# Four scatters of a batch at one place in GpSimd's order, instead of three and one

## What is computed

```python
h = layernorm(x) * (1 + ca) + sa
Q, gate, K, V = h @ Wq ..., h @ Wk, h @ Wv        # 16 heads of 8 features, Q and K RMS-normed
attn = softmax(Q K^T / sqrt(8));  o = (attn @ V) * sigmoid(gate)
x = x + ga * (o @ Wo + bo)
h = layernorm(x) * (1 + cb) + sb
rw = softmax(h @ router_w.T);  vals, idx = top_k(rw, 2)      # 2 of 32 experts for each token
x = x + gb * sum_k vals_k * (h @ expert_weights[idx_k])
```

## Time and profile before

| | |
|---|---|
| median of three runs | 1137.25 us |
| the profiled execution | 1129.86 us |
| its span, first to last instruction | 1128.2 us |
| first part of the program (attention and routing) | to about 780 us |
| busy over the span: TensorE, VectorE, ScalarE, GpSimd | 60%, 66%, 48%, 52% |
| mean granted TensorE clock | 0.845 of full speed |

### The profile page before, as it was taken

One profiled execution on the slowest core, in us unless ns is written; L12 is line 12 of the kernel. 1 busy time (PEld: TensorE's weight loads), 2 busy tenths in 40 slices (PEclk: granted clock), 3 DMA queues, 4 the chain that ended last, 5 costly groups with the idle time before them and its releaser, 6 DMA issues. The chain is left out here.

```text
span 1128.2 us, 26188 instructions
## 1 busy us (share of the span) xinstructions
PE 675.7 (60%) x5838; PEld 432.4 (38%) x5839; DVE 741.2 (66%) x2260; ACT 536.6 (48%) x1335; POOL 584.1 (52%) x940
## 2 busy tenths in 40 slices
PE   2477887878888788788888888761356660000000
PEld 0134555545545445454455555430345550000000
DVE  5486998898898898889888889634622222333333
ACT  1255876677777777677677777640022220000000
POOL 4121456555655655665565655556222226666765
PEclk9588999899999998999999999965599995555555
DMA  2245545344544544545454453310666563333333
GB/s 60 62 127 130 128 116 143 93 114 113 133 110 106 137 113 104 128 104 124 109 124 110 113 133 99 86 43 28 227 201 203 204 194 90 98 102 94 106 98 95
DMA packets 115825, 132.72 MB, mean 118 GB/s; under 512 B 16901, under 2 KB 96613, under 8 KB 115269
## 3 DMA queue, kind: packets, MB, share of 16 engines
q1 hardware_dynamic: 96036, 91.93, 32.0%
q0 software_dynamic: 12736, 33.84, 9.4%
q10 hardware_dynamic: 7008, 6.43, 2.0%
HBM read 78.62 MB, written 52.96 MB: 117 GB/s over the span
## 5 line engine op out<-in xcount | busy, mean ns | idle before, releaser
L1144 DVE TENSOR_REDUCE negmax<-mx_ps 128x2 f32<-128x512 f32 x512 | 340.2, 684 | 77.6 <-remote 41.0
L892 ACT ACTIVATE pr<-st_ps 128x512 f32<-128x512 f32 x512 | 286.7, 597 | 51.3 <-PE st_ps L1536 45.5
L1514 PE MATMUL mx_ps<-k_aug,q_aug 126*128 126x256 bf16 x1024 | 203.4, 283 | 74.4 <-DVE negmax L1144 58.2
L1536 PE MATMUL st_ps<-q_aug,k_aug 128*128 128x256 bf16 x1024 | 176.6, 281 | 0.9 <-ACT pr L892 0.3
L1550 PE MATMUL o_ps<-pr,v_aug 128*32 128x256 f32 x2048 | 141.2, 394 | 48.0 <-ACT oT L898 25.9
L781 POOL DMA_INDIRECT yg<-ys_d,gi x128 | 124.3, 971 | 63.1 <-issue 41.1
L713 POOL DMA_INDIRECT xs_d<-h,slot x128 | 127.7, 998 | 55.6 <-DVE slot L1267 32.0
L1514 PEld LDWEIGHTS mx_ps<-k_aug,q_aug 126*128 126x128 bf16 x1024 | 77.0, 99 | 176.8 <-issue 168.2
L1536 PEld LDWEIGHTS st_ps<-q_aug,k_aug 128*128 128x128 bf16 x1024 | 96.5, 103 | 35.1 <-issue 11.8
L1550 PEld LDWEIGHTS o_ps<-pr,v_aug 128*32 128x32 f32 x2048 | 56.8, 110 | 98.1 <-issue 78.1
L1416 DVE TENSOR_SCALAR yw<-yg,p_all 128x128 f32<-128x128 f32 x64 | 16.1, 310 | 113.1 <-DMA yg<-ys_d,gi 87.4
(11 more groups left out here) (188 smaller groups left out, 1317.5 us busy)
## 6 DMA issues: line engine op xcount, KB each, us to landing
q_aug<-q_d SPq DMA_DIRECT2D x64, 192.0 KB
ys_d<-ys POOLq DMA_DIRECT2D x48, 256.0 KB, 3.0
mod_o<-mod_d SPq DMA_DIRECT2D x32, 256.0 KB
bias_p<-bias_d SPq DMA_DIRECT2D x32, 200.0 KB
q_d<-parts SPq DMA_DIRECT2D x32, 192.0 KB, 2.1
k_d<-parts SPq DMA_DIRECT2D x32, 192.0 KB, 2.1
k_aug<-k_d SPq DMA_DIRECT2D x64, 96.0 KB
xs<-xs_d ACTq DMA_DIRECT2D x48, 128.0 KB, 2.2
```

Of the source, the lines that this page charges most:

```text
L892: nc.scalar.activation(pr[:, h % PR], st_ps[score_bank(b, h)][:], ACT.Exp, scale=SCALE).then_inc(exp_d, 1)
L1144: v.tensor_reduce(negmax[:, :, h], mx_ps[h % 2][:], AX.X, ALU.max, negate=True).then_inc(mx_d, 1)
L1514: last = t_.matmul(mx_ps[h % 2][:, qc], q_aug[b.par][0:MROW, h, qc * P:(qc + 1) * P], k_aug[b.par][0:MROW, h, :], start=True, stop=True)
L1536: last = t_.matmul(st_ps[score_bank(b, h)][:, kc], k_aug[b.par][:, h, kc * P:(kc + 1) * P], q_aug[b.par][:, h, :], start=True, stop=True)
```

## The change

All four scatters of a batch are issued at one place of GpSimd's step, one step after their slots are known, right behind `low_part(b1)`. Before, the first three stood behind `max_rest` of the batch's own step, and the fourth at the very start of the next. Only GpSimd's list changes; the lists of the other engines are the same.

```diff
             def step(b0, b1, b2, b3, b4, b5, b6, b7, b8):
 
-                scatter(b7, 3)
                 copy_v(b2)
                 x_plus_bias(b4)
                 scale_wo(b4)
                 low_part(b1)
+                scatter(b7, 0)
+                scatter(b7, 1)
+                scatter(b7, 2)
+                scatter(b7, 3)
                 keep_slot(b7)
                 scale_wqkv(b0)
                 chosen(b6)
...
                 max_rest(b2)
-                scatter(b6, 0)
-                scatter(b6, 1)
                 keep_weights(b8)
-                scatter(b6, 2)
                 less_largest(b6)
                 norm_qk(b0, 0)
                 norm_qk(b0, 1)
```

## The result

| | median, us | lowest to highest | runs |
|---|---|---|---|
| before | 1137.94 | 1133.21 to 1139.79 | 4 |
| after | 1206.55 | 1204.02 to 1211.17 | 4 |

The ratio is 1.0614 (95% interval 1.0568 to 1.0661): 68.6 us slower. The prediction said 1174 us, 36 us slower, with a range of 1146 to 1218. The sign and the range held; the value was only half of the loss. The experiments were timed in three groups, each beside the kernel before on a chip of its own (medians of 1053.73, 1128.15 and 1128.18 us), and each ratio is to the kernel before of the same group.

The account below looks back on a forecast made before the run. VectorE was taken as nearest to a bound, with 2.6 us idle per step. Per step +3.0 - 0.2 - 1.6 + 0.2 = +1.4 us, over 26 steps +36: 1137.25 + 36 = 1174 us, range 1146 to 1218.

Parts of the forecast that it names:

- The fourth scatter leaves the start: Step start on GpSimd, ahead of `v_aug`: moving this scatter away is worth 0, between 0 and 0.1 us a step.
- The mask is late by 3.0: Four scatters behind the low part start GpSimd's mask 3.0 us late (2.8 to 3.8); TensorE's count and later work move too.
- The 0.2 won back: Of the mask's 3.0 us delay, 0.2 a step is recovered from VectorE's 0.65 us idle elsewhere (bounds 0 and 0.65).
- The end stop's gain of 1.6: Step end: moving three scatters away removes the 1.8 to 1.95 us stop, gaining 1.6 us a step (0 to 1.95).
- a sign of being wrong: Listed sign against the forecast: "remote" waits of 1.8 us still there, at the old place or beside the train.
- The rival that saw it coming: End stop stays or moves along with the scatters: +3.0 to +3.3 us a step, 1219 us; chance 0.20.
- The clock, +0.2: TensorE's longer pause lowers its clock more often: 0.2 us a step added, between -0.3 and 1.5.
- the clock falls in nearly every step: Rival: TensorE spends 3.4 to 6.9 us per step at the lower clock, 0.5 to 1.4 more, 1200 us; chance 0.13.
- the one with 0.52: The forecast itself: +1.4 us a step over 26 steps, 1174 us, within 1160 to 1190; chance 0.52.
- a mean clock under 0.90: Sign that the clock's term was too small: TensorE's mean clock in 200 to 640 us below 0.90.
- the faster rival: Mask hardly late and end stop gone: 1095 us with no delay, about 1135 with half of it; chance 0.08.

## Why the prediction was half right

The step falls into two stretches: from the low part's end to the mask, and from the mask round to the next low part's end. The first is the median of the traces, the second what the step leaves.

| kernel | low part to mask | mask to next low part | step, us |
|---|---|---|---|
| before | 3.0 | 18.5 | 21.5 |
| before, additions for scatters | 3.0 | 17.2 | 20.2 |
| after | 5.95 | 18.55 | 24.5 |
| after, additions for scatters | 5.9 | 18.25 | 24.2 |
| after, TensorE kept busy | 5.95 | 17.0 | 23.0 |

- *The fourth scatter leaves the start: 0.* Right: moving it alone gave 0.997, a few us at most.
- *The mask is late by 3.0.* Right in place and size: 5.93 against 3.03 us, and TensorE waits 3.7 us a step for it. At full clock nearly all of it enters the step: 22.97 (TensorE kept busy) less 20.19 is 2.8, the holding included. The 0.2 won back were fair.
- *The end stop's gain of 1.6.* The size stands between the 1.3 that the additions give at the least and 2.0 at the most. The mechanism was not the forecast's: the stop left the step's end, but it was not removed, it moved. Results are now held beside the train, 2.9 us a step for `onT` (55.9 in 19 cases), where TensorE and nearly all others wait for the mask anyway. By the prediction's own list that was a sign of being wrong. The rival that saw it coming priced it at 1219 us, as if the held results would cost in full at the new place too; the traces give them 0.3, not clear of noise.
- *The clock, +0.2.* This is the term that was mis-sized, and most of the missing half. The prediction put it so: "I add 0.2 us a step, between -0.3 and 1.5". It measured 1.5 a step between two traces, 1.2 between two medians and 1.0 between two ratios, near the upper bound. The table shows how it hid the gain: without the stop, mask to low part would be 17.0 to 17.2 us; the half clock behind the pause puts it back to 18.55, as long as before with the stop.

With the terms of the traces: 2.5 for the late mask at full clock (2.8 less the 0.3), 0.3 for the holding, 1.5 for the clock, 1.3 of gain: 2.5 + 0.3 + 1.5 - 1.3 = +3.0, and 24.50 - 21.51 is 2.99. They must add up so, since each term is a difference between the same steps; the sum divides the loss and doesn't check it. With a gain of 2.0 the late mask and the holding would have 3.5 together, and the clock would keep its 1.5. The kernel before loses something to the clock too (0.96 to 0.97); that share lies within the gain. A check from outside is the forecast's sum with the clock of the medians, 1.4 - 0.2 + 1.2 = 2.4 a step: 26 times that is 62 us, and the medians stand 68.6 apart, 2.6 a step. The first two profiled executions, 1129.86 and 1207.40 us, stand 77.5 apart; their steps, (702.8 - 162.4) / 25 = 21.62 and 24.34 us, make 68 of it over the 25 steps between masks.

That the range held is in part luck: the sum gave 36 us and steps of 22.7 to 23.4 us, where the traces have 24.3 to 24.5, and its upper end came from the prices of the rivals. Of the cases laid out, the one that came true is "the clock falls in nearly every step", at 1200 us and 0.13, and not the one with 0.52. The row for it was there: in the step of the earlier trace rows with the clock at 0.85, a pause of 1.9 us was followed by the fall, and I took the price of a longer pause from the average over all steps. I should have asked what TensorE does while it waits: in the kernel before it stops at the step's end for less than 2 us with work on either side, after the change it stands for 3.7 us in each step, and then the low clock lies on the matmuls that release everyone. The sign that the prediction gave for this, a mean clock under 0.90, was set wrongly too: the mean is 0.91, since the longer step dilutes 3.3 us at 0.52.

The Trainium skill, page "TensorE: Matmul & The Clock Gate", section "Why this matters for your kernels", warns against such pauses between bursts of matmuls. The runs agree: 0.91 with the pause and 1.00 with the same wait filled, 24.50 and 22.97 us a step. The Trainium skill, page "DMA: Bandwidth & Descriptors", section "Anatomy of one DMA — SWDGE (gpsimd) path", calls the making of descriptors small; on GpSimd's row each indirect DMA is 0.95 to 1.03 us and the next one comes 1.26 to 1.34 us later, and the faster rival that leaned on it fell with that.

## What to carry to other kernels

Room on an engine is a pocket ahead of one instruction, with a size: 2.1 us took one scatter for nothing, and four overran it by 2.9, which nearly all entered the step, since TensorE's list had no slack behind the mask. When a change makes TensorE wait in each step, add to the wait itself what the low clock costs behind it (here 1.0 to 1.5 us on top of 2.8), and read it from a stretch at the low level, not from an average; a few matmuls without use in the wait gave it back here. A stand-in for an instruction has neighbours of its own: look at what the other engines' instructions beside it take before its step is used as a base. And when a stall is taken away, ask which buffers, landings or held results wait at the new place: both this change and the spread of the scatters took the stop from the step's end and met waits elsewhere.

## What was not expected of the hardware

- While a train of indirect DMAs is issued on GpSimd, results of TensorE reach ScalarE and VectorE late (transposes issued at 529.51, copied at 533.16), with waits that no instruction accounts for. GpSimd additions of 1.29 to 1.48 us at the same places show none. Three close together at the step's end did it, and four behind the low part; moving the fourth alone left the stop where it was, and four set apart show none of these waits of `oT`, `onT` or `negmax`. How it comes about, the traces don't say.
- One chip ran the kernel before in 1053.73 us, the others in 1128 to 1138. Of these 75 us some 20 lie behind the pipeline: with the additions at the old places, the stretch from the last mask to the end took 335.2 us there (732.4 to 1067.6) and 355.5 on the chip with 1128.18 us (727.7 to 1083.2), where the program gathers rows with 128 indirect DMAs. The rest, about 54 us, is 2.1 a step over 26 steps. Without scatters the steps are close on both, 20.16 us there with the long additions and 20.19 here with the short ones, so much of the rest may belong to the scatters; there is no trace of the kernel before from that chip, and it stays open.
- Additions of 128x600 on GpSimd took 1.46 to 1.48 us and of 128x520 1.29 to 1.30 us, and with them VectorE's `n<-r` took 828 ns (short) and 1344 ns (long) instead of 218. In one step with short additions it ran from 413.23 to 414.05 beside an addition that ended at 413.97.
